# First stage of a two-layer kernel: a fifth place for weights, TensorE by two chunks, part of the exponentials' shifts on VectorE

## What is computed

```python
def _L0_conv_ref(x, accumulators):                # x is the group-normalised input here
    log_w = log_softmax(log(accumulators), axis=2)         # accumulators: 1024 positions x 128 x 128
    x_max, w_max = ...                                     # maxima over the channels
    prod = einsum('vhbk,vhks->vhbs', exp(xs - x_max), exp(log_w - w_max))
    return log(prod) + x_max + w_max                       # back to images first

x = x + _L0_conv_ref(_gn(x), accumulators)
x = x + _L1_conv_ref(_gn(x), ...)                 # attention over 1024 tokens, image by image
```

## Time and profile before

| | |
|---|---|
| median of 3 runs | 1115.49 us (1114.75 to 1117.63) |
| the profiled execution's own time | 1115.15 us |
| its span, from the first to the last instruction | 1113.4 us |
| outside the span in that execution | 1.7 us |
| busy in the span: PE, ACT, DVE, POOL | 1036.8, 913.2, 804.3, 535.0 us |
| read from HBM, written | 136.45, 20.83 MB |
| first stage, from the first product to the last | 56.23 to 217.86 us of the span |

### The profile page before, as it was taken

One profiled execution on the slowest core, in us unless ns is written; L12 is line 12 of the kernel. 1 busy time (PEld: TensorE's weight loads), 2 busy tenths in 40 slices (PEclk: granted clock), 3 DMA queues, 4 the chain that ended last, 5 costly groups with the idle time before them and its releaser, 6 DMA issues.

```text
span 1113.4 us, 19843 instructions
## 1 busy us (share of the span) xinstructions
PE 1036.8 (93%) x7160; PEld 785.8 (71%) x7160; DVE 804.3 (72%) x1389; ACT 913.2 (82%) x1708; POOL 535.0 (48%) x267
## 2 busy tenths in 40 slices
PE   1299999868999999999999999999999999999996
PEld 0055555446887777777777777777777778887774
DVE  7723555578777777777777777777777777777767
ACT  1799999447888888888888888888888888888885
POOL 0045455413355555555555555555555555555534
PEclk9999999979999999999999999999999999999998
DMA  8999999630122222222222222212222212222212
GB/s 356 403 354 419 413 405 414 273 150 20 58 77 77 77 76 77 76 77 77 97 112 97 96 104 106 96 77 87 84 89 85 76 77 77 77 78 77 77 58 96
DMA packets 33265, 158.60 MB, mean 142 GB/s; under 512 B 4248, under 2 KB 4876, under 8 KB 22924
## 3 DMA queue, kind: packets, MB, share of 16 engines
q1 hardware_dynamic: 33164, 157.29, 36.7%
HBM read 136.45 MB, written 20.83 MB: 141 GB/s over the span
## 4 chain that ended last, share of the span: by engine, by line
PE 83%; DMA 7%; DVE 4%; ACT 2%; issue 2%; POOL 1%; SPq 1%; POOLq 0%; ACTq 0%; DVEq 0%
PE PS L1244 22%; PE PS L1245 21%; PE PS L1246 21%; PE PS L1262 5%; PE PS L1219 4%; PE PS L1209 4%; DMA Wt<-acc 4%; PE PS L1230 2%; DMA X<-x 2%; PE PS L1256 2%; PE PS L1250 1%; DVE st L775 1%; SPq L299 1%; DMA NU<-factor_rows 0%; ACT PS L617 0%
## 5 line engine op out<-in xcount | busy, mean ns | idle before, releaser
L957 DVE TENSOR_TENSOR Pl<-PS,Ph 128x512 fp32r<-128x512 f32 x512 | 347.9, 690 | 185.5 <-ACT PS L617 180.9
L616 ACT ACTIVATE Ph<-PS 128x512 fp32r<-128x512 f32 x384 | 234.3, 610 | 96.1 <-PE PS L1246 93.2
L617 ACT ACTIVATE PS<-PS 128x512 f32<-128x512 f32 x512 | 305.2, 610 | 9.4 <-PE PS L1246 9.4
L1244 PE MATMUL PS<-Ph,hh 128*128 128x512 f32 x512 | 206.7, 404 | 1.0 <-DVE Pl L957 1.0
L1244 PE MATMUL PS<-uTh,nTh 128*128 128x512 f32 x512 | 200.3, 391 | 0.9 <-DVE uTl L931 0.9
L1245 PE MATMUL PS<-Pl,hh 128*128 128x512 f32 x512 | 200.3, 391 | 0.0
L1246 PE MATMUL PS<-Ph,hl 128*128 128x512 f32 x512 | 200.0, 391 | 0.0
L1246 PE MATMUL PS<-uTh,nTl 128*128 128x512 f32 x512 | 199.9, 390 | 0.0
L1245 PE MATMUL PS<-uTl,nTh 128*128 128x512 f32 x512 | 199.8, 390 | 0.0
L428 POOL TENSOR_TENSOR hl<-X,hh 128x1024 fp32r<-128x1024 f32 (+1 forms) x33 | 77.3, 2342 | 196.6 <-ACT hh L601 170.8
L411 POOL TENSOR_TENSOR LL<-LL 128x512 f32<-128x512 f32 x64 | 82.6, 1290 | 134.5 <-ACT LL L505 134.5
(11 more groups left out here) (145 smaller groups left out, 1601.8 us busy)
## 6 DMA issues: line engine op xcount, KB each, us to landing
Wt<-acc SPq DMA_DIRECT2D x64, 1024.0 KB, 7.4
out<-X SPq DMA_DIRECT2D x37, 512.0 KB, 2.6
X<-x SPq DMA_DIRECT2D x16, 1024.0 KB, 19.6
SQ<-norm_rows SPq DMA_DIRECT2D x31, 512.0 KB, 3.6
X<-factor_rows SPq DMA_DIRECT2D x31, 512.0 KB, 3.9
NU<-factor_rows SPq DMA_DIRECT2D x31, 512.0 KB, 4.9
X<-out SPq DMA_DIRECT2D x7, 512.0 KB, 5.7
out<-X SPq DMA_DIRECT2D x4, 256.0 KB, 2.1
```

The source lines that it names most:

```text
L616: act.activation(Ph[:, g % RING, :], sl, ACT.Exp, scale=SHARP)
L617: act.activation(sl, sl, ACT.Exp, scale=SHARP).then_inc(weights_ready, 1)
L957: dve.tensor_tensor(Pl[:, r, :], SL[r], Ph[:, r, :].bitcast(F32), ALU.subtract)\
L1244: pe.matmul(out_, lh, rh, start=start, stop=False)
```

## The change

Four things change, all in the first stage.

1. The weights of chunk 0 are loaded into LL, which holds nothing until logs(0) is written, and logs(0) waits for the products of chunk 0 anyway. The chunks 1 to 63 use the four rooms of Wt in turn. So five loads are issued without a wait, and the load of chunk ch waits for the products of chunk ch - 4 from the sixth chunk (ch = 5) on. As before, four rooms turn over after that.
2. TensorE goes by two chunks: sums(c), products(c), sums(c + 1), transposes(c - 2), transposes(c - 1), products(c + 1), for even c. The last two transposes stand behind the last products.
3. Of the eight images of a pair of chunks VectorE shifts the last two (`shifts`, two instructions of 128 x 128 on VectorE), and ScalarE takes their exponentials in one instruction of 128 x 256 without scale and bias. ScalarE's order for a pair is now: five exps, logs(c), one exp, the exponential of the two shifted images, logs(c + 1).
4. VectorE goes by two chunks as well: the two shifts, then both additions of the pair before, then its four pieces of statistics. The pieces of chunks 62 and 63 now stand ahead of the additions of these chunks.

```diff
--- before.py
+++ after.py
@@ -42,6 +42,8 @@
 BY_ACT = (13, 17, 23, 25)
 ACT_UPTO = (0, 2, 4)
 AT_ONCE = 5
+IPP = 2 * B // GCH
+SHIFTS = 2
 
 
 TT = NPOS // P
@@ -163,6 +165,7 @@
         bound_summed = sem("bound_summed")
         flag_ready = sem("flag_ready")
         image_loaded = [sem(f"image_loaded{i}") for i in range(LOADS)]
+        first_weights_loaded = sem("first_weights_loaded")
         weights_loaded = [sem(f"weights_loaded{i}") for i in range(WS)]
         stat_pieces = sem("stat_pieces")
         act_steps = sem("act_steps")
@@ -238,6 +241,11 @@
         NCONST = 9
         block = ctx.enter_context(nc.Block())
 
+        def weights_of(c):
+            if c == 0:
+                return LL[:, :, :, :].rearrange("p u t (i s) -> p (u t i) s", s=C)
+            return Wt[:, (c - 1) % WS, :, :]
+
         def sums_of(i):
             return W1 if i == 4 else W0
 
@@ -299,10 +307,10 @@
                 sp.dma_start(X[:, i * IPL:(i + 1) * IPL, :],
                              x[:, i * IPL:(i + 1) * IPL, :]).then_inc(image_loaded[i], 16)
             for ch in range(NCH):
-                if ch >= WS:
+                if ch > WS:
                     sp.wait_ge(products_ready, ch - WS + 1)
-                sp.dma_start(Wt[:, ch % WS, :, :], acc[ch, :, :].rearrange("k (i s) -> k i s", s=C))\
-                    .then_inc(weights_loaded[ch % WS], 16)
+                sp.dma_start(weights_of(ch), acc[ch, :, :].rearrange("k (i s) -> k i s", s=C))\
+                    .then_inc(weights_loaded[(ch - 1) % WS] if ch else first_weights_loaded, 16)
 
             def spill(i):
                 sp.dma_start(out[B - AWAY + i, :, :], room[i]).then_inc(spilled[i], 16)
@@ -549,13 +557,20 @@
             images = ET[:, 0, hi - AT_ONCE:hi, :]
             act.activation(images, images, ACT.Exp).then_inc(exps_ready, AT_ONCE)
             per = B // GCH
-            for c in range(NCH):
+            for c in range(0, NCH, 2):
                 g, i = divmod(c, GCH)
+                images = range(i * per, i * per + IPP)
                 if g + 1 < NGR:
                     if i == 0 and g:
                         act.wait_ge(products_ready, GCH * g)
-                    exps(g + 1, range(i * per, (i + 1) * per))
+                    exps(g + 1, images[0:5])
                 logs(c)
+                if g + 1 < NGR:
+                    exps(g + 1, images[5:IPP - SHIFTS])
+                    act.wait_ge(shifted, AT_ONCE + SHIFTS * (c // 2 + 1))
+                    late = ET[:, (g + 1) % 2, images[IPP - SHIFTS]:images[-1] + 1, :]
+                    act.activation(late, late, ACT.Exp).then_inc(exps_ready, SHIFTS)
+                logs(c + 1)
 
             def token_squares(b):
                 if b == 0:
@@ -878,6 +893,8 @@
                 xc = X[:, :, c * CP:(c + 1) * CP].rearrange("p b (q j) -> p b q j", j=CJ)
                 dve.tensor_tensor(xc, TR[c % 2].rearrange("p (j q b) -> p b q j", j=CJ, q=Q), xc, ALU.add)\
                     .then_inc(x_added, 1)
+
+            def pieces_of(c):
                 m, i = divmod(c, per)
                 if m:
                     if i == 0:
@@ -885,8 +902,26 @@
                     for b in range(i * ipc, (i + 1) * ipc):
                         piece(1, m - 1, b)
 
-            for c in range(NCH - 1):
-                add_logs(c)
+            def shifts(c):
+                g, i = divmod(c, GCH)
+                if i == 0 and g:
+                    dve.wait_ge(products_ready, GCH * g)
+                last = i * B // GCH + IPP
+                for b in range(last - SHIFTS, last):
+                    dve.tensor_scalar(ET[:, (g + 1) % 2, b, :], X[:, b, (g + 1) * GP:(g + 2) * GP], RS[:, b:b + 1],
+                                      NB[:, b:b + 1], ALU.mult, ALU.add).then_inc(shifted, 1)
+
+            for c in range(0, NCH, 2):
+                if c < NCH - GCH:
+                    shifts(c)
+                if c:
+                    add_logs(c - 2)
+                    add_logs(c - 1)
+                    pieces_of(c - 2)
+                    pieces_of(c - 1)
+            pieces_of(NCH - 2)
+            pieces_of(NCH - 1)
+            add_logs(NCH - 2)
 
             def last_pieces(lo, hi):
                 for b in range(lo, hi):
@@ -1201,23 +1236,26 @@
                     sum_groups(i, h)
 
             def sums(c):
-                u, slot = c % 2, c % WS
-                pe.wait_ge(weights_loaded[slot], 16 * (c // WS + 1))
+                u, w = c % 2, weights_of(c)
+                if c:
+                    pe.wait_ge(weights_loaded[(c - 1) % WS], 16 * ((c - 1) // WS + 1))
+                else:
+                    pe.wait_ge(first_weights_loaded, 16)
                 if c >= 2:
                     pe.wait_ge(logs_ready, c - 1)
                 for q in range(Q):
                     pe.matmul(PS[32 * q:32 * q + 32, 2 * u + 1, :], ones[:, :],
-                              Wt[:, slot, q * CJ:(q + 1) * CJ, :].rearrange("k i s -> k (i s)"), start=True, stop=True)
+                              w[:, q * CJ:(q + 1) * CJ, :].rearrange("k i s -> k (i s)"), start=True, stop=True)
 
             def products(c):
-                u, slot = c % 2, c % WS
+                u, w = c % 2, weights_of(c)
                 g, i = divmod(c, GCH)
                 if i == 0:
                     pe.wait_ge(exps_ready, B * (g + 1))
                 for j in range(CJ):
                     for q in range(Q):
                         last = pe.matmul(PS[32 * q:32 * q + 32, 2 * u, j * C:(j + 1) * C],
-                                         ET[:, g % 2, :, i * CP + q * CJ + j], Wt[:, slot, q * CJ + j, :],
+                                         ET[:, g % 2, :, i * CP + q * CJ + j], w[:, q * CJ + j, :],
                                          start=True, stop=True)
                 last.then_inc(products_ready, 1)
 
@@ -1230,15 +1268,18 @@
                     last = pe.transpose(TR[u][:, j * C:(j + 1) * C], LL[:, u, 0, j * C:(j + 1) * C], ident[:, :])
                 last.then_inc(transposed, 1)
 
-            for c in (0, 1):
+            for c in range(0, NCH, 2):
                 sums(c)
-            for c in range(NCH + 2):
-                if 2 <= c < NCH:
-                    sums(c)
-                if c >= 2:
+                if c == 0:
+                    sums(1)
+                products(c)
+                if c:
+                    sums(c + 1)
                     transposes(c - 2)
-                if c < NCH:
-                    products(c)
+                    transposes(c - 1)
+                products(c + 1)
+            transposes(NCH - 2)
+            transposes(NCH - 1)
 
             def three(out_, lh, ll, rh, rl, start=True, stop=True):
                 pe.matmul(out_, lh, rh, start=start, stop=False)
```

## The result

| | before | after |
|---|---|---|
| median of 20 runs each | 1115.12 us (1112.64 to 1119.10) | 1117.96 us (1114.44 to 1123.26) |
| the profiled execution's own time, its span | 1115.15, 1113.4 us | 1117.28, 1115.5 us |

The ratio is 1.0026, 95% interval 1.0014 to 1.0037. The change costs 2.8 us. The prediction said 1113.5 us, and 1117.96 lies over the end of its range, 1116.6. The forecast, a gain of 2 us, had a chance of 0.50 there; the case that came, rival C, slower, had 0.08.

What follows compares the result with a forecast made beforehand. The prediction took DMA to bound the first stage, PE and ACT within 2%. Gains of 1.25 (fifth room) and 0.7 less a loss of 0.3 (end) made 1.65 us off 1115.15, so 1113.5 us, range 1109.8 to 1116.6.

Steps and rivals of the forecast that it cites:

- rival C: First stage: odd chunks' rooms, held longer, get their loads late; 6 us lost, 1119.5 us, chance 0.08.
- The bound: First stage: DMA, PE and ACT within 2% of one another, DMA slowest at 2.53 us a chunk.
- The fifth room: First stage's start: a fifth load without a wait shortens the transfers' rest by 1.6 us, less 0.35; gain 1.25 us.
- the gap: The DMA engines' only rest in the first stage, 54.5 to 58.4 us; 3.9 us, to become 2.3.
- TensorE's pair: TensorE's new order in the first stage: two chunks in 4.75 us against DMA's 5.06; nothing on the path.
- ScalarE and VectorE: First stage: fewer exponentials on ScalarE, two shifts more on VectorE; nothing on the path, with 0.4 us of cover.
- The end: End of the first stage: TensorE loses 0.3 us, VectorE gains 0.7 from two pieces moved ahead of the last addition.
- The sign to look for: A DMA share clearly under 1 mid-stage would show rival C; idle time before sums over 6.4 us, the forecast.

Runs made afterwards that it cites:

- e10: The change with TensorE's old order and the sums left out from chunk 2 on, 1114.43 us, 0.9992 of before.
- e1: The kernel before with only the fifth room (part 1) added, 1114.06 us, 0.9995 of before.
- e12: The change with both sets of transposes ahead of the odd sums and without the fifth room, 1113.81 us, 0.9992 of before.
- e11: The change with one of the two sets of transposes moved behind the odd products, 1114.47 us, 0.9988 of before.
- e13: The kernel before with odd chunks' rooms held about 1.5 us longer, by a wait for later transposes, 1131.64 us, 1.0132 of before.
- e3: The kernel before with only the ScalarE and VectorE parts (3 and 4) added, 1113.94 us, 0.9997 of before.
- e8: The change without part 2, so with TensorE's order of before, 1113.50 us, 0.9986 of before.
- e2: The kernel before with only TensorE's order by two chunks (part 2) added, 1123.55 us, 1.0070 of before.
- e4: The change with both sets of transposes moved ahead of the odd sums, 1112.98 us, 0.9982 of before.
- e9: The change with TensorE going by single chunks, transposes ahead of sums and products, 1117.24 us, 1.0012 of before.

## Why the prediction was wrong, point by point

**The bound.** Right, as far as it can be told: the transfers set the floor, and e10's 2.54 us stands beside the 2.53 of the prediction. That they lead PE isn't shown: from 72 to 122 us before ran at 420 GB/s with PE busy for 49.98 of 50 us, so there the two were level. The sentence from the Trainium skill, "DMA: Bandwidth & Descriptors", section "Where 436 GB/s comes from", of 358 GB/s for a core, disagrees with the trace after as well (426 from 54 to 56).

**The fifth room.** Neither shown nor refuted: 1.25 us forecast, 0.8 and 1.2 between medians. In the profiled execution after, chunk 7 is 1.07 us ahead of before, and by the rates from 54 to 72 us 0.24 MB more had been moved, 0.6 us of transfers; but with the room alone, in e1's, its sums start at 72.08, no sooner than before's 71.97. The steps to it depend on the execution. In the profiled one after, the first products were slow (start, duration, line, count):

```profile
56.13 1.72 PE L1257 MATMUL PS<-LL,ET 128*32 128x128 f32 x28
57.62 1.93 PE L1257 MATMUL PS<-Wt,ET 128*32 128x128 f32 x32
...
60.31 1.04 PE L1257 MATMUL PS<-Wt,ET 128*32 128x128 f32 x32
```

The clock column says 1.00 there, but 1.9 us is nearly twice 1.04. The room isn't the reason: e12, with four rooms, has them as slow. Chunk 5's load was issued at 59.61, not 58.28, and the gap ran from 56.9 (0.47 x 2 us after 56) to 60.7 (0.83 x 4 us ahead of 64): as long as before, 3.8 us, with one load more done ahead of it. In e11's execution the same products took 1.1 us each, and its gap ran from 57.1 to 59.3 (shares 0.54 and 0.36), 2.2 us where 2.3 were forecast.

**TensorE's pair.** This is the step that failed. Its time was right: from 64.09 to 68.76 PE waited for nothing, and the pair took 4.67 us, against 4.68 to 4.96 forecast:

```profile
64.09 1.05 PE L1247 MATMUL PS<-Wt,ones 128*32 128x512 f32 x8
64.95 1.06 PE L1257 MATMUL PS<-Wt,ET 128*32 128x128 f32 x32
65.83 1.05 PE L1247 MATMUL PS<-Wt,ones 128*32 128x512 f32 x8
66.81 1.09 PE L1268 MATMUL PS<-ident,LL 128*128 128x128 f32 x8
67.83 1.11 PE L1257 MATMUL PS<-Wt,ET 128*32 128x128 f32 x32
68.76 1.05 PE L1247 MATMUL PS<-Wt,ones 128*32 128x512 f32 x8
```

The conclusion "nothing on the path", since PE is faster than DMA, was wrong. It compared two rates, and the order of the work inside the pair decided: how long a landed chunk keeps its room. Rival C had this with all its numbers (3.1 us held, 6.9 left for the landing, 2.63 us a chunk; measured 3.23 held, 7.26 for the landing, 2.63). It was set aside by "three loads in flight at 2.5 us make 7.5 by themselves, so most of the 7.4 is queueing, which shrinks when issues come later". e13 refutes that sentence: later by 1.5 us, the landing shrinks by 0.3. And the least landing of 5.0 was taken for what a later issue could reach, where it belongs to the first load behind the gap, whose 16 engines ended within 0.6 us of one another. C's 6 us for 59 chunks came out as 4.56 for 56; with 1.07 at the start and 0.5 at the end on the other side 3.0 us are left, close to the 2.8 of the medians.

**ScalarE and VectorE.** Right, as far as it can be measured: nothing on the path (e3, e8). The exponential of 256 columns takes 0.41 us (forecast 0.35 to 0.45), the shifts 0.34. What the prediction did not see is that without part 3 part 2 would have cost far more (e2).

**The end.** Right in kind. VectorE's last work (before: the earlier trace rows):

```profile
221.58 2.70 DVE L790 BATCH_NORM_STATS2 st<-X 128x6 f32<-128x256 f32 x8
224.19 1.49 DVE L894 TENSOR_TENSOR X<-PS,X 128x512 f32<-128x512 f32 x2
225.72 1.41 DVE L790 BATCH_NORM_STATS2 st<-X 128x6 f32<-128x256 f32 x4
227.16 0.19 DVE L815 TENSOR_REDUCE gsum<-st 128x4 f32<-128x32 f32 x1
```

Four pieces, 1.41 us, stand behind the last additions in place of six, 2.05. From the last products' start to the reduction it is 6.46 us in place of 6.98: 0.52 gained, where 0.7 was forecast. TensorE's loss of 0.3 can't be seen apart from the wait for the last weights (0.81 us before the sums of chunk 63).

**The sign to look for** was wrong too: C was to show as a DMA share clearly under 1. It showed as 0.99 to 1.01 with 394 to 411 GB/s. And one sign of being right came with C as well: idle time before the sums over 6.4 us, mostly before odd ones. Where the rate went can be counted in the records of single packets, 72 to 212 us, per engine. Packets of 8 KB that took over 0.35 us (0.31 is usual) number 210, before 104, and took 5.1 us more than usual, before 2.3. The time that is missing to 16 packets under way comes to 1.6 us, before 0.25. Both together are 4.1 us more than before; the fall from 414 to 403 GB/s is worth 3.9 of 140 us. In e13 the same sum gives 16.3 for 16.1. So two thirds of the loss are slow packets, which the DMA share counts as busy. I read them as queues that had run empty and start again; which engine a packet belongs to is not in the records, so that reading, and why the engines' spread holds at 2.2 us, stays open.

## What to carry to other kernels

Where a ring of buffers is filled at the pace of the memory, an order of work is judged by how long a landed buffer is held, not only by whether the consumer is faster than the transfers: work that doesn't read the buffer belongs ahead of the wait for it, not between the first and the last read (e4, two lines, 5 us), as long as that work doesn't itself have to wait there (e9). Take the landing time for such a ring from the crowded part of the trace, where the last of 16 engines counts, not from the fastest load seen, until a run has shown that it shrinks. Read GB/s beside the DMA share: 1 in the latter was found at 394 GB/s and at 420.

## What had not been expected of the hardware

- A 1 MB load that meets idle engines lands in 4.7 to 5.0 us; with its neighbours in flight it never came under 5.8 us in e13's stage, median 7.0 for its odd chunks, though some engine had its part done 4.4 us after the issue.
- The busy share of the DMA engines was 0.95 at 355 GB/s and 1.01 at 420.
- The first two products of the stage took 1.0 us each in some executions and 1.9 in others, with the clock column at 1.00 in both.
- The sums ran into the products in 0.86 to 0.88 us where nothing stood between, as against 0.97 to 1.00 ahead of transposes; eight transposes took 1.02 us, where two sets of four take 2 x 0.59.
